# A graph layer's edge loop in 41 steps of 24 dense and 16 gathered tiles, with strip columns as wide as each tile's nodes

## What is computed

```python
h = relu(layernorm(x))
deg = maximum(zeros(n).at[dst].add(1.0), 1.0)
edge_weight = (deg[src] * deg[dst]) ** -0.5
edge_msg = relu(edge_attr @ W1e + b1e) @ W2e + b2e
messages = (h[src] + edge_msg) * edge_weight[:, None]
agg = segment_sum(messages, dst, num_segments=n)
combined = (1.0 + gin_eps) * h + agg
out = relu(combined @ W1n + b1n) @ W2n + b2n + h
out = out * rsqrt(mean(out * out, -1) + eps) * rms_w
return x + out
```

## Time and profile before

| | |
|---|---|
| median of 3 runs | 1082.5 us (1081.37 to 1082.73) |
| profiled execution: its time | 1078.76 us |
| profiled execution: its span | 1076.9 us |
| mean granted TensorE clock | 0.993 |
| busy: PE, PEld, DVE, ACT, POOL | 962.5, 795.8, 910.1, 652.7, 756.9 us |
| first pair of counts starts; last window addition | 96.4 us; 1024.5 us |

### The profile page before, as it was taken

The page is one execution under the profiler, slowest core; times in us unless marked ns, Lnnn a source line. Parts: engine busy times, 40 slices in busy tenths (PEclk is TensorE's granted clock), DMA queues, the critical chain, the costliest instruction groups (busy, mean ns, idle before and its releaser), DMA issues. The chain is left out here.

```text
span 1076.9 us, 35614 instructions
## 1 busy us (share of the span) xinstructions
PE 962.5 (89%) x12752; PEld 795.8 (74%) x12752; DVE 910.1 (85%) x4063; ACT 652.7 (61%) x1747; POOL 756.9 (70%) x754
## 2 busy tenths in 40 slices
PE   0324999999999999999999999999999999999985
PEld 0323788888888887887887888788788788888753
DVE  6998888888888878888887888887888898888668
ACT  7962666666666666656665666665666566666435
POOL 2045777777777777777777777777777777777475
PEclk9999999999999999999999999999999999999988
DMA  6045544544544544454454454454445445442483
GB/s 239 15 176 178 167 127 138 162 130 137 163 131 138 155 139 142 140 152 144 122 170 137 128 167 130 139 152 140 141 141 154 142 126 168 142 123 75 159 298 104
DMA packets 57741, 156.99 MB, mean 146 GB/s; under 512 B 16052, under 2 KB 23399, under 8 KB 57185
## 3 DMA queue, kind: packets, MB, share of 16 engines
q1 hardware_dynamic: 33776, 104.43, 27.9%
q0 software_dynamic: 22784, 47.07, 18.4%
q10 hardware_dynamic: 1008, 3.21, 0.9%
HBM read 147.95 MB, written 6.70 MB: 144 GB/s over the span
## 5 line engine op out<-in xcount | busy, mean ns | idle before, releaser
L1063 POOL DMA_INDIRECT arena<-node_rows,idx x712 | 712.4, 1001 | 228.9 <-issue 139.9
L1234 ACT ACTIVATE arena<-bank 128x294 f16<-128x294 f32 x900 | 328.5, 422 | 266.3 <-PE bank L1139 260.0
L1224 ACT ACTIVATE arena<-bank 128x512 f32<-128x512 f32 x405 | 222.6, 596 | 104.8 <-PE bank L1089 98.5
L1149 PE MATMUL bank<-t_words,arena 128*120 128x256 f16 x2205 | 282.6, 275 | 0.4 <-DVE arena L1352 0.4
L1289 DVE TENSOR_SCALAR arena<-iota_c,code 128x294 f16<-128x294 f16 x900 | 273.7, 359 | 2.3 <-PE bank L1139 2.3
L1302 DVE SCALAR_TENSOR_TENSOR arena<-iota_h,hi_f,bank 128x49 f32<-128x49 f32 x900 | 184.1, 261 | 61.9 <-PE bank L1104 59.9
L1149 PEld LDWEIGHTS bank<-t_words,arena 128*120 128x120 f16 x2205 | 233.8, 133 | 0.6 <-issue 0.6
L1139 PE MATMUL bank<-arena 128*128 128x294 f16 x900 | 206.1, 307 | 23.2 <-DVE arena L1289 17.7
L1089 PEld LDWEIGHTS bank<-w1e,arena 64*128 64x128 f32 x3240 | 215.6, 190 | 4.7
L1089 PE MATMUL bank<-w1e,arena 64*128 64x128 f32 x3240 | 218.1, 272 | 0.0
L1139 PEld LDWEIGHTS bank<-arena 128*128 128x128 f16 x900 | 101.4, 144 | 84.7 <-DVE arena L1289 35.4
(11 more groups left out here) (208 smaller groups left out, 802.5 us busy)
## 6 DMA issues: line engine op xcount, KB each, us to landing
arena<-in_attr SPq DMA_DIRECT2D x90, 512.0 KB
arena<-low_src SPq DMA_DIRECT2D x47, 652.5 KB, 7.5
arena<-node_rows,idx POOLq DMA_INDIRECT x712
arena<-in_attr SPq DMA_DIRECT2D x45, 128.0 KB
node_rows<-arena SPq DMA_DIRECT2D x1, 3160.5 KB, 8.9
arena<-in_x ACTq DMA_DIRECT2D x7, 448.0 KB, 11.0
arena<-in_x SPq DMA_DIRECT2D x6, 512.0 KB, 12.4
out<-arena SPq DMA_DIRECT2D x12, 224.0 KB
```

The lines of the kernel that those rows point to most:

```text
L1063: nc.gpsimd.indirect_dma_start(out=edge_rows[:, u, j, 0:ROW], out_offset=None, in_=table, in_offset=bass.IndirectOffsetOnAxis(ap=idx[:, c, ...
L1149: mm = nc.tensor.matmul(x_sum[0:XC, 0:2 * D], strip[:, u, k, :], T16[:, k, :], start=k == 0, stop=k == NBLK - 1)
L1224: nc.scalar.activation(out.rearrange("p (j o) d -> p o j d", o=2), z[:, :, j0:j0 + n // 2, :], ACT.Relu).then_inc(r_ready, 1)
L1234: nc.scalar.activation(strip[:, u, :, tile * W:tile * W + W], pair_bank[:, j * 512:j * 512 + CW].rearrange("p (k w) -> p k w", w=W), ACT.C ...
```

## The change

- A step takes 24 dense and 16 gathered tiles, in 41 steps; 28 of them are one gathered tile short. All five phases have two units.
- The 12 pairs are counted in the order `FIRST_PAIR`, `MORE_PAIRS`: phases 3 and 4 count three pairs, with the spread products cut in two around the one in the middle. Looks are 2, 2, 2, 3, 3 pairs by phase. `LB`, the tiles in one low one-hot build, is 6.
- A dense tile takes as many columns of the strip as its destination nodes span. The strip has 128 columns (`XS`). GpSimd works out the starts (`column_at`) in the prologue by a running sum; ScalarE reads each tile's start into a register ahead of the copy. The copy still writes 6 columns, and the tile after it writes over those that aren't its own, so a copy also waits for the pair before.
- `edge_rows` keeps two sets of fetched rows, but one of relu results, between them.
- The windows are 112 (dense) and 88 (gathered) nodes wide.
- The prologue loads the tiles' last nodes (`tails`, `slots`), checks spans with them, works out the columns, turns them to every partition by products with ones, and clears the strip.

```diff
-WIN = 96
+WD, WG = 112, 88
+
+
+TD, TG = 24, 16
 TS = TD + TG
-LOOKS = [0, 2, 4, 6, 8, 10]
-UNITS_D = [(0, 4), (4, 4), (8, 4), (12, 4), (16, 4)]
+LOOKS = [0, 2, 4, 6, 9, 12]
+UNITS_D = [(0, 4), (4, 4), (8, 4), (12, 4), (16, 4), (20, 4)]
 UNITS_G = [(0, 4), (4, 4), (8, 4), (12, 4)]
 UD, UG = len(UNITS_D), len(UNITS_G)
 U = UD + UG
-PHASES = [(0, 1), (2, 3), (4, 5), (6, 7), (8,)]
+PHASES = [(0, 1), (2, 3), (4, 5), (6, 7), (8, 9)]
 NPH = len(PHASES)
-SPREAD_AT = [0, 10, 12, 27, 42, 49]
+SPREAD_AT = [0, 11, 13, 32, 48, 49]
+FIRST_PAIR = [1, 3, 5, 8, 11]
+MORE_PAIRS = [(2,), (4,), (6, 7), (9, 10), ()]
 UL = TD // 2
 RL = 2
 PB = 3
-GROUP_AT = [0, 5, 10, 15]
+GROUP_AT = [0, 6, 12, 18]
...
-XC = TD * W
-NPASS = -(-N // W)
+XS = 128
+WSAFE = W - 1
+NPASS = -(-N // WSAFE)
 NA = TD // 2
-LB = 10
+LB = 6
...
+            step(nc.gpsimd.tensor_tensor(in_rows(widths[:, 0, :]), tails_s, heads_s, ALU.subtract))
+            step(nc.gpsimd.tensor_scalar(widths[:, 0, :], widths[:, 0, :], float(W - 1), 1.0, ALU.min, ALU.add))
+            step(nc.gpsimd.memset(widths[:, 0, NA - 1:NA], float(W)))
+            a = 0
+            for by in (1, 2, 4, 8, 16):
+                nc.gpsimd.tensor_copy(widths[:, 1 - a, 0:by], widths[:, a, 0:by])
+                step(nc.gpsimd.tensor_tensor(widths[:, 1 - a, by:TD], widths[:, a, by:TD], widths[:, a, 0:TD - by], ALU.add))
+                a = 1 - a
+            nc.gpsimd.tensor_tensor(in_rows(head_at[:, :]), heads_s, slots[:, 0, 0:1].unsqueeze(1).broadcast_to((S, 2, NA)), ALU.subtract)
+            step(nc.gpsimd.tensor_copy(starts[:, 1:TD + 1], widths[:, a, :]))
+            pool.sem_inc(starts_ready, 1)
...
+            step(nc.gpsimd.tensor_tensor(starts[:, :], beyond_safe[:, :], fast[0:S, 0:1].broadcast_to((S, TD + 1)), ALU.mult))
+            nc.gpsimd.tensor_tensor(head_at[:, :], head_at[:, :], fast[0:S, 0:1].broadcast_to((S, TD)), ALU.mult)
+            step(nc.gpsimd.tensor_tensor(starts[:, :], starts[:, :], safe_starts[:, :], ALU.add))
+            nc.gpsimd.tensor_copy(column_at[:, :], starts[:, :])
+            step(nc.gpsimd.tensor_tensor(head_at[:, :], head_at[:, :], starts[:, 0:TD], ALU.subtract))
+            step(nc.gpsimd.tensor_tensor(jumps[:, 0:TD - 1], head_at[:, 1:TD], head_at[:, 0:TD - 1], ALU.subtract))
+            own_step = ident[0:S, 0:S].unsqueeze(2).broadcast_to((S, S, TD))
+            for a, of in ((0, starts[:, 1:TD + 1]), (1, jumps[:, :])):
+                nc.gpsimd.tensor_tensor(spread_out[:, a, :, :], own_step, of.unsqueeze(1).broadcast_to((S, S, TD)), ALU.mult).then_inc(columns_ready, 1)
...
+                    nc.gpsimd.memset(strip_words, 0.0).then_inc(strip_clear, 1)
...
+            step(nc.vector.scalar_tensor_tensor(out=rel_s[:, :, :].rearrange("p s t -> p (s t)"), in0=dst_e, scalar=-0.5, in1=tails.bitcast(I32),
+                                                op0=ALU.add, op1=ALU.is_gt, accum_out=extreme[:, 1:2]))
+            v.wait_ge(starts_ready, 1)
...
+            v.wait_ge(columns_turned, 1)
+            passed = code[:, :, :].rearrange("p s t -> p (s t)")
+            step(nc.vector.tensor_scalar(passed, bank2[0][:, 0:S * TD], part_f[:, 0:1], None, ALU.is_le))
+            step(nc.vector.tensor_tensor(passed, passed, bank2[1][:, 0:S * TD], ALU.mult))
+            step(nc.vector.tensor_reduce(off[:, 0, :], code[:, :, :], AX.X, ALU.add))
+            nc.vector.tensor_scalar(off[:, 0, :], off[:, 0, :], part_f[:, 0:1], None, ALU.add)
...
+def row_at(u):
+
+    return u * (ROW + D)
+
+
+def r_at(c):
+
+    return (1 - c % 2) * D
...
-                                pool.wait_ge(tile_ps, 2 * (after + 6))
+                                pool.wait_ge(tile_ps, 2 * (after + 7))
                             else:
-                                pool.wait_ge(strip_ready, 2 * (after + 5))
+                                pool.wait_ge(strip_ready, 2 * (after + 6))
...
-                    mm = nc.tensor.matmul(x_sum[0:XC, 0:2 * D], strip[:, u, k, :], T16[:, k, :],
+                    mm = nc.tensor.matmul(x_sum[:, 0:2 * D], strip[:, u, k, :], T16[:, k, :],
...
-                        count_pair(c, u, 2 * p + 1)
+                        count_pair(c, u, FIRST_PAIR[p])
                     if live(c + 1):
                         look(c + 1, p)
+                    more = MORE_PAIRS[p] if live(c) else ()
                     if c == S and p == 0:
                         spread_rows(c - 1, 1 - u, 0, NBLK)
-                    elif c < S and live(c - 1) and SPREAD_AT[p] < SPREAD_AT[p + 1]:
-                        spread_rows(c - 1, 1 - u, SPREAD_AT[p], SPREAD_AT[p + 1])
+                    elif c < S and live(c - 1):
+                        k0, k1 = SPREAD_AT[p], SPREAD_AT[p + 1]
+                        half = (k0 + k1) // 2 if len(more) > 1 else k1
+                        spread_rows(c - 1, 1 - u, k0, half)
+                        if len(more) > 1:
+                            count_pair(c, u, more[0])
+                            spread_rows(c - 1, 1 - u, half, k1)
+                    elif len(more) > 1:
+                        count_pair(c, u, more[0])
                     if live(c - 2) and p == 0:
                         window_gathered(c - 2)
                         window_dense(c - 2)
                     if live(c - 1) and last:
                         turn(c - 1)
-                    if live(c) and not last:
-                        count_pair(c, u, 2 * p + 2)
+                    if more:
+                        count_pair(c, u, more[-1])
...
-                    if not (isinstance(c, int) and c < 2):
-                        act.wait_ge(summed_g, (c - 2) * UG + (k - UD + 1))
-                    out = edge_rows[:, u, first:first + n, ROW:XW]
+                    if not (isinstance(c, int) and c < 1):
+                        act.wait_ge(summed_g, (c - 1) * UG + (k - UD + 1))
+                    out = edge_rows[:, first:first + n, ROW:ROW + D]
...
+                    first = act.value_load(column_at[c:c + 1, j * NA + p:j * NA + p + 1], min_val=0, max_val=XS - W)
                     act.wait_ge(tile_ps, 2 * (c * NA + p) + (j + 1))
+                    if p > 0:
+                        act.wait_ge(strip_ready, 2 * (c * NA + p - 1) + (j + 1))
                     if p == 0 and j == 0 and not (isinstance(c, int) and c < 2):
                         act.wait_ge(x_ps, c - 1)
-                    tile = 2 * p + j
-                    nc.scalar.activation(strip[:, u, :, tile * W:tile * W + W],
+                    nc.scalar.activation(strip[:, u, :, bass.ds(first, W)],
...
-                        if p > 0:
-                            keep_counts(c, u, 2 * p)
-                        relu(c, u, 2 * p)
-                        if p < NPH - 1:
-                            relu(c, u, 2 * p + 1)
-                        keep_counts(c, u, 2 * p + 1)
+                        for q in MORE_PAIRS[p - 1] if p > 0 else ():
+                            keep_counts(c, u, q)
+                        for k in PHASES[p]:
+                            relu(c, u, k)
+                        keep_counts(c, u, FIRST_PAIR[p])
...
-                    else:
-                        pairs_ahead(c, u, 2 * p + 2)
+                    for q in MORE_PAIRS[p]:
+                        pairs_ahead(c, u, q)
...
-                        pairs_ahead(c + 1, 1 - u, 1)
-                    elif 2 * p + 3 < NA:
-                        pairs_ahead(c, u, 2 * p + 3)
+                        pairs_ahead(c + 1, 1 - u, FIRST_PAIR[0])
+                    else:
+                        pairs_ahead(c, u, FIRST_PAIR[p + 1])
```

More of the change, by code:

```diff
@@ L905, in look_of, with phase_of @@
 def look_of(pair):
-    return pair // UL * NPH + pair % UL // 2 + 1
+    return pair // UL * NPH + phase_of(pair % UL) + 1
+def phase_of(k):
+    return sum(k >= first for first in LOOKS[1:])
 def low_set(c, p):
@@ L923, in steps, with encode @@
         one(c, c % 2)
-def encode(nc, part, code, hi_f, rel_d, inside, step):
+def encode(nc, part, code, hi_f, rel_d, wide, inside, step):
     if part == 0:
@@ L932, in encode @@
     if part == 1:
-        step(nc.vector.scalar_tensor_tensor(out=inside, in0=rel_d[:, :, :], scalar=float(W), in1=inside, op0=ALU.is_lt, op1=ALU.mult))
+        step(nc.vector.scalar_tensor_tensor(out=inside, in0=rel_d[:, :, :], scalar=wide[:, 0:1], in1=inside, op0=ALU.is_lt, op1=ALU.mult))
     if part == 2:
```

222 lines of the change are left out of this document (138 added, 84 removed).

## The result

The changed kernel takes 1175.97 us (median of 4 runs, 1174.97 to 1176.88) beside 1082.62 us for the kernel before on the same chip: ratio 1.084, 95% interval 1.081 to 1.087. The sign was forecast; the size was 93 us instead of 32, and above the range. The profiled execution spans 1173.2 us, 96.3 more than before.

The account below looks back on a forecast made before the run. GpSimd's gathers set the middle stretch, with TensorE's own period 0.4 us below. 38 steps of 23.05 us less 42 of 20.43, plus 15 fixed, gave +32.7 us; forecast 1114.5 us, range 1068 to 1140.

Parts of the forecast that it names:

- The estimate of 21.2 us without waits: TensorE's step: 19.73 us without waits, plus 1.5 us for four more dense tiles.
- The slow path: Rival in which columns don't fit and the slow path runs; given no chance.
- the waits of phases 3 and 4: TensorE at the third pair waits 0.41 us in each phase for ScalarE's copies, plus 0.07 at phase 4's last pair.
- a copy's length: ScalarE's copy into the strip, taken as 0.42 us long (mean 422 ns).
- the prologue: Work before the steps: more VectorE passes, GpSimd's products and the mask's wait; +8.5 us together, between 3 and 13.
- filling: Before the steady steps: two steps without waits at +1.5 us and four more looks, +4 us.
- (c): Rival: ScalarE's load is slower than VectorE's by 0.16 us; +0.5 us a step, 1134 us; chance 0.11.
- (f): Rival: each load takes 0.3 us more than counted; 24.2 us a step, 1158 us; chance 0.03.
- (a): Rival: copies keep up, waits of phases 3 and 4 vanish; 21.5 us a step, 1056 us; chance 0.17.
- (b): Rival: half the waits; 22.2 us a step, 1083 us; chance 0.09.
- (d): Rival: VectorE takes over as the pace-setter of the steps, +0.9 us, 1149 us; chance 0.06.
- The break-even period: Step period at which the change costs nothing, with +15 us fixed outside the steps: 22.19 us.

Follow-up runs that it names:

- fixed starts: Changed kernel with column starts fixed at 5 x tile in the program, so no register loads or address operations: 1126.61 us, ratio 1.041.
- loads ahead: Changed kernel with both register loads of a pair ahead of the pair's first wait, and no bounds check behind a load: 1128.19 us, ratio 1.059 or 1.043 unspecified.
- products moved: Changed kernel with its 49 spread products put 3, 6, 18, 18, 4 by phase: 1146.89 us alone, 1086.29 us with both loads ahead and unchecked.
- the run with even starts: Changed kernel with each strip column start rounded down to an even number, loads and waits kept: 1165.28 us, ratio 1.077.
- the best run: Changed kernel with loads ahead and unchecked, spread products moved, and prologue DMAs, mask and strip clearing rearranged: 1081.00 us, ratio 0.9992.

## Where the prediction was right and wrong

**Right.** TensorE waits before second tiles for ScalarE's copies; GpSimd has gaps; no wait for gathers; VectorE idles 79.4/20.7 = 3.8 us a step; loads of 0.3 us; the clock. The estimate of 21.2 us without waits stands within what the runs can tell: 24.20 less 3.8 of waits before pairs (45.5 and 33.9 us in 20.7 steps) is 20.4, 22.01 less 1.3 is 20.7, and some waits were in 21.2 already. The slow path did not run.

**Wrong: the waits of phases 3 and 4** ("the copies behind relus: seen at +1.65 and +1.95", "wait 0.41 in each, plus 0.07 at phase 4's last pair"). Two steps of this failed. I let the relus hide both loads of the first pair and put the copies behind them 0.31 us apart; only the first load is hidden, and the second copy begins 0.55 us after the first (0.30 with fixed starts, 0.32 with loads ahead). So the third pair's second tile goes on at +2.20 and +2.17, not at +1.95. And I priced each wait from the pair before it, and never laid the copies of a whole phase end to end. The third pair's first copy starts 0.7 us after its pair and not 0.49, because its load, issued one at a time, waits for the copies ahead; from there the chain goes on 0.7 to 0.8 us apart, and the phase's last pair waits 0.17 and 0.42 us on average for which I had nothing and 0.07. The sixth copy begins at +4.6, where I had TensorE in the next phase since +3.60 and +3.46. Together that is 0.3 and 0.5 us more than counted in these two phases. Fixed starts gave back 1.1 us a step, loads ahead and products moved 2.2, so the chain is shown to be the cause.

**Wrong: a copy's length.** 0.42 us was true for even starts, and all starts of the kernel before are multiples of 6. 379 of 984 take 0.62, which costs 0.23 us a step by the run with even starts, part of the excess above. No row of before could show it.

**Wrong, by 10 us: the prologue.** The passes, the products and the mask's wait (4 counted, 4.9 measured) were right. Missing were landings of DMAs (L527 starts at 16.26 us, its counterpart L447 at 9.83, of which 1.0 was counted as slot operations; the slots and 820 KB of tails share the queue, which is likely the reason) and L691, blocked until GpSimd's memset had ended (+2.9). I had set the memset down as hidden. The Trainium skill, "SBUF — State Buffer", section "SBUF: two separate sides", says that VectorE and GpSimd share a port pair as an exclusive lock: a VectorE instruction in a two-port mode, or one with two SBUF inputs against a GpSimd instruction that reads SBUF, is blocked for the whole of a GpSimd instruction that began first. This trace agrees: the memset began first (74.07), and from its end, 79.43, to the end of L691, 80.30, is 0.87 us, about the instruction's own 1.07. That L691 runs in a two-port mode no run here shows. That rule would have given the term.

**Wrong, by 8 us: filling.** I gave two steps 1.5 us each and some looks, "without waits". They have the copy chain too; at 3.77 us a step they would be 7.5, with the looks 8.5; measured +12.0, and the other 3.5 us are open.

**The rivals.** (c) and (f) gave the loads more time, and (f)'s 24.2 us a step is what came; but its reason is wrong, a load takes 283 ns. That its step came out right is luck. The Trainium skill, "DMA: Bandwidth & Descriptors", section "Latency and other measured facts", gives a floor of about 600 ns for such a load; all 984 on ScalarE disagree (270 to 318 ns). (a), (b) and (d) did not happen. The break-even period was 22.19 with 15 us fixed; with the 34.8 measured it is (858.2 - 34.8)/38 = 21.67, and the best run stands at 22.0 with a fixed part of 24.5, which puts its break-even at (858.2 - 24.5)/38 = 21.94: hence no difference.

**Open:** what ails the chip on which the kernel before takes 1355 us, and why loads cost 86 us there and 4 here; how the 1.1 us of loads ahead divide between the missing check and the order of the loads; what held 4 of the 984 loads back by 0.29 us.

## What to carry to other kernels

Where an engine's instructions each need a register load of their own, lay all of a phase end to end at the full spacing (here 0.71 us for a 0.42 us copy) and compare that with what the other engine has to do; pricing wait by wait misses the chain. A load is cheap while there is slack before its wait: 20 a step cost 0.4 to 0.7 us with room, 24 cost 1.1 without. If two engines pass a bank back and forth, work that depends on neither belongs between the passes, and fewer steps are worth less than their period once the fixed part has grown.

## What the runs showed that I had not expected

- ScalarE's copies of six 2-byte columns, 49 runs to a partition, take 420 ns, but 616 where the start is odd and the six cross a multiple of eight columns (16 bytes): 379 of 984, none of the others.
- A register load on ScalarE (283 ns) is shorter than on VectorE (304). Of the 738 loads that stand behind another copy, 614 begin within 0.02 us of that copy's start, 120 earlier, while it still waits for the engine, and 4 later by 0.29. Behind two relus the load begins before the second of them does. The check behind a load is 152 ns more of register work, and without it two copies stand 0.23 us closer.
- VectorE's L691 took 3.98 us beside GpSimd's memset and 1.07 with the strip cleared elsewhere; a small addition took 1.89 instead of 0.20 beside a GpSimd product.
- The same kernel took 1083 us on some chips and 1355 on another, at equal lengths of the instructions compared (263 and 261 ns).
